# Two chunks' gates of steps 1 to 4 as seven block products, and the matrix operands kept in device memory by product

## What is computed

```python
state = prop_state
for _ in range(5):
    s_in = state @ in_W.T + in_b
    s_out = state @ out_W.T + out_b
    a_in = Af @ s_in
    a_out = AfT @ s_out
    a = concatenate([a_in, a_out, state], axis=-1)
    r = sigmoid(a @ r_W.T + r_b)
    z = sigmoid(a @ z_W.T + z_b)
    joined = concatenate([a_in, a_out, r * state], axis=-1)
    h_hat = tanh(joined @ h_W.T + h_b)
    state = (1.0 - z) * state + z * h_hat
out = tanh(state @ o1_W.T + o1_b) @ o2_W.T + o2_b
return layernorm(x + out)
```

## Time and profile before

| | |
|---|---|
| median of 3 runs | 1029.72 us (1029.61 to 1030.45) |
| the profiled execution, its own time | 1030.75 us |
| its span in the trace | 1028.9 us |
| TensorE busy | 98% of the span, 4648 matmuls |
| VectorE busy | 58% |
| ScalarE busy | 39% |
| share of the chain that ended last that is TensorE | 92% |
| mean granted TensorE clock | 0.99 of full |

### The profile page before, as it was taken

One profiled execution on the slowest core, in us unless ns is written; L12 is line 12 of the kernel. 1 busy time (PEld: TensorE's weight loads), 2 busy tenths in 40 slices (PEclk: granted clock), 3 DMA queues, 4 the chain that ended last, 5 costly groups with the idle time before them and its releaser, 6 DMA issues.

```text
span 1028.9 us, 11463 instructions
## 1 busy us (share of the span) xinstructions
PE 1005.5 (98%) x4648; PEld 458.5 (45%) x4648; DVE 592.3 (58%) x933; ACT 403.8 (39%) x544; POOL 38.7 (4%) x43
## 2 busy tenths in 40 slices
PE   6999999999999999999999999999999999999995
PEld 3444444444444444444444444444444444444443
DVE  4999968895354338544433674353347534446756
ACT  3656665542144126413421552143135314322443
POOL 0311000000000000000000000000000002001100
PEclk8999999999999999999999999999999999999998
DMA  9998991327430244333003642410344335001101
GB/s 330 389 411 344 396 343 33 77 65 218 151 136 0 103 166 91 72 143 143 1 1 143 189 72 72 169 73 0 143 154 72 62 143 189 1 1 42 42 1 41
DMA packets 87236, 134.30 MB, mean 131 GB/s; under 512 B 60432, under 2 KB 75408, under 8 KB 78992
## 3 DMA queue, kind: packets, MB, share of 16 engines
q1 hardware_dynamic: 84880, 125.19, 35.8%
q0 software_dynamic: 2304, 8.39, 2.1%
HBM read 102.11 MB, written 16.78 MB: 116 GB/s over the span
## 4 chain that ended last, share of the span: by engine, by line
PE 92%; DVE 3%; ACT 2%; DMA 1%; issue 1%; SPq 1%; ACTq 0%; DVEq 0%
PE bank L1260 42%; PE bank L1173 36%; PE bank L1116 11%; PE bank L1292 1%; DMA tmp<-in_adj 1%; PE bank L1273 1%; DMA xop_words<-pq_words 0%; SPq L270 0%; DVE pq_words L810 0%; ACT pq_words L468 0%; DVE pq_words L1012 0%; DVE areg L957 0%; ACT pq_words L554 0%; ACT tmp L476 0%; DVE tmp L704 0%
## 5 line engine op out<-in xcount | busy, mean ns | idle before, releaser
L1173 PE MATMUL bank<-areg,xop_words 128*128 128x512 fp8e4 x1792 | 390.1, 379 | 1.4 <-DVE pq_words L1012 1.1
L1260 PE MATMUL bank<-pq_words,w 128*128 128x512 f16 x1440 | 327.3, 379 | 0.0
L1173 PEld LDWEIGHTS bank<-areg,xop_words 128*128 128x128 f16 x1792 | 174.5, 98 | 214.7 <-DVE pq_words L1012 3.1
L1260 PEld LDWEIGHTS bank<-pq_words,w 128*128 128x128 f16 x1440 | 140.9, 98 | 169.9 <-DVE pq_words L1038 0.2
L476 ACT ACTIVATE tmp<-bank,bias_sb,scal 128x512 f32<-128x512 f32 x120 | 93.1, 776 | 201.4 <-PE bank L1260 201.4
L554 ACT ACTIVATE pq_words<-pq_words 128x512 f16<-128x512 f32 x48 | 30.2, 630 | 236.8 <-DVE pq_words L1024 140.5
L831 DVE SCALAR_TENSOR_TENSOR bank<-deg_words,vdeg,bank 128x512 f32<-128x512 f16 x120 | 90.0, 752 | 51.8 <-ACT bank L490 50.7
L1260 PE MATMUL bank<-split,w 128*128 128x512 f16 x480 | 116.7, 379 | 2.4 <-issue 1.9
L1116 PE MATMUL bank<-areg,xop_words 128*128 128x512 fp8e4 x512 | 113.5, 385 | 3.7 <-ACT areg L421 3.7
L490 ACT ACTIVATE bank<-deg_words,vdeg 128x512 f32<-128x512 f16 x120 | 82.7, 691 | 5.2 <-DVE deg_words L794 1.5
L1116 PEld LDWEIGHTS bank<-areg,xop_words 128*128 128x128 f16 x512 | 50.7, 99 | 66.0 <-issue 7.4
(11 more groups left out here) (132 smaller groups left out, 602.9 us busy)
## 6 DMA issues: line engine op xcount, KB each, us to landing
areg<-kept_operands SPq DMA_DIRECT2D x32, 1792.0 KB, 10.6
tmp<-in_adj SPq DMA_DIRECT2D x16, 1024.0 KB, 7.0
tmp<-in_adj_t SPq DMA_DIRECT2D x16, 1024.0 KB, 8.3
kept_operands<-xop_words POOLq DMA_DIRECT2D x11, 512.0 KB, 8.2
areg<-in_x SPq DMA_DIRECT2D x8, 512.0 KB, 8.1
kept_operands<-areg SPq DMA_DIRECT2D x4, 1024.0 KB, 10.2
kept_operands<-tmp POOLq DMA_DIRECT2D x5, 512.0 KB, 3.3
pq_words<-in_gate_w SPq DMA_DIRECT2D x6, 384.0 KB, 6.2
```

The costliest lines, as they stand in the source:

```text
L1173: last = nc.tensor.matmul(dst[:, :], xop[:, m // 2, operand_block(xo, part, m % 2), :], slot8[g % 2][:, m, mo, :], start=first and m == pa ...
L1260: last = nc.tensor.matmul(dst[:, :], w16[:, k, wp, feat(gi)], rhs, start=False, stop=i == KT - 1 and (wp, xp) == PASSES[-1], skip_group_ch ...
```

## The change

For steps 1 to 4, the gates of chunks 0 and 1 are no longer computed tile by tile. Features and chunks make a 2 x 2 block product per gate and direction, which is done as seven products (`pair_gate`, `pair_product`): the left operands are blocks of the gate weights and four sums of them (`ws`), the right ones are `y11`, `y21`, `y22` and the four sums `t1` to `t4` of the y blocks (`yop`). The state's part stays as it was (`pair_state`). `degree_differences`, `weight_full`, `weight_sums`, `weight_hi` and `weight_lo` prepare the sums of the weights and degrees once, in step 1. The scales of all operands change by a factor of 4, and the degree terms with them. Chunks 2 and 3, and step 0, keep the old form; the first seeds of chunk 2 now stand in group 3 of every step.

In `kept_operands` each operand of a group is now one piece of 512 KB, stored in pieces of 512 bytes (the sums with two DMAs for each one before, the rows with three for each two). There is one place for each of the seven operands instead of two slots; SP loads the next group's operand into it when the product that read it has ended. The freed slot holds `yop` and the late chunks' y.

The diff, cut to its core:

```diff
-Y_SPLIT = {False: {"y22": 1, "y12": 2, "y11": 3, "y21": 4}, True: {"y11": 1, "y22": 2, "y12": 3, "y21": 4}}
+Y11, Y21, Y22, YT1, YT2, YT3, YT4 = range(7)
+Y_ORDER = {0: ("y11", "y22", "t1", "t3", "t2", "y21", "t4"), 1: ("y22", "t3", "y11", "t1", "t2", "y21", "t4"),
+           2: ("y22", "y12", "y11", "y21"), 3: ("y22", "y12", "y11", "y21")}
+Y_BASE = (0, 7, 14, 18)
+Y_STEP = 22
+Y_PLACE = {"y11": Y11, "y21": Y21, "y22": Y22, "t1": YT1, "t2": YT2, "t3": YT3, "t4": YT4}
+PAIR_TILES = ((0, 0), (0, 1), (1, 1), (1, 0))
...
-        kept = nc.dram_tensor("kept_operands", (2 * 2, P, PAIRS, NX * CW // 4), F32, kind="Internal").ap()
+        pair_banks = (bank[4:8], (bank_a, bank_b, bank_e, bank_c), bank[4:8])
+        kept = nc.dram_tensor("kept_operands", (2 * 2, NX, P, PAIRS, CW // 4), F32, kind="Internal").ap()
...
+            def load_operand(at, mo, done):
+                if at > 0:
+                    sp.wait_ge(done, at)
+                sp.dma_start(place_w[:, mo, :, :], kept[at % 4][mo]) \
+                    .then_inc(s_place[mo], 16)
+            def load_group(at):
+                load_operand(at, M11, s_p1)
+                load_operand(at, MT2, s_p6)
+                load_operand(at, MT1, s_p5)
+                load_operand(at, MT3, s_p7)
+                load_operand(at, M22, s_p3)
+                load_operand(at, M21, s_p2)
+                load_operand(at, MT4, s_p4)
...
             for t in range(1, STEPS):
-                for g in range(4):
-                    at = 4 * (t - 1) + g
-                    if at + 2 < 4 * LAST:
-                        sp.wait_ge(s_p4, at + 1)
-                        load_group(t + (g + 2) // 4, (g + 2) % 4)
+                for at in range(4 * (t - 1) + 1, 4 * t + 1):
+                    if at < 4 * LAST:
+                        load_group(at)
...
-                to = kept.rearrange("(h d) p m w -> d p h m w", d=2)[d][:, :, m, MT1 * CW // 4:]
                 pool.wait_ge(s_t, i + 1)
-                if i < RING_A:
-                    nc.gpsimd.dma_start(to, ring_a[:, i % 3, :].rearrange("p (h w) -> p h w", h=2)) \
...
+                for h in range(2):
+                    to = kept[2 * h + d, MT1:MT1 + 4, :, m, :].rearrange("s p w -> p s w")
+                    if i < RING_A:
+                        rows = ring_a[:, i % 3, :].rearrange("p (h s w) -> p h s w", h=2, s=4)
+                        nc.gpsimd.dma_start(to, rows[:, h]).then_inc(s_kept_a[i % 3], 16)
...
+            def weight_hi(d):
+                act.wait_ge(s_wsum, 3 * d + 3)
+                nc.scalar.copy(ws[:, d, :, 0, :], w_sums).then_inc(s_wsh, 1)
...
+            def weight_full(d):
+                k = FT * (1 - d)
+                if d == 0:
+                    dve.wait_ge(s_gate, GT * CH)
+                else:
+                    dve.wait_ge(s_wsh, 1)
+                nc.vector.tensor_tensor(w_full, w16[:, k:k + FT, 0, :], w16[:, k:k + FT, 1, :], ALU.add) \
+                    .then_inc(s_wfull, 1)
+            def weight_sums(d):
+                w = w_full.rearrange("p k (r f m) -> p k f r m", r=3, f=FT)
+                a11, a12, a21, a22 = w[:, 0, 0], w[:, 1, 0], w[:, 0, 1], w[:, 1, 1]
+                s1, s2, s3, s4 = [w_sums[:, i, :].rearrange("p (r m) -> p r m", r=3) for i in range(4)]
+                dve.wait_ge(s_wfull, d + 1)
+                nc.vector.tensor_tensor(s1, a21, a22, ALU.add).then_inc(s_wsum, 1)
+                nc.vector.tensor_tensor(s3, a11, a21, ALU.subtract)
+                dve.wait_ge(s_wsum, 3 * d + 1)
+                nc.vector.tensor_tensor(s2, s1, a11, ALU.subtract).then_inc(s_wsum, 1)
+                dve.wait_ge(s_wsum, 3 * d + 2)
+                nc.vector.tensor_tensor(s4, a12, s2, ALU.subtract).then_inc(s_wsum, 1)
+            def weight_lo(d):
+                dve.wait_ge(s_wsh, d + 1)
+                nc.vector.tensor_tensor(ws[:, d, :, 1, :], w_sums, ws[:, d, :, 0, :], ALU.subtract) \
+                    .then_inc(s_wsl, 1)
...
+            def degree_differences():
+                v = vdeg.rearrange("p d (r f) -> p d f r", f=FT)
+                nc.vector.tensor_tensor(vdif[:, :, 0, :], v[:, :, 0, :], v[:, :, 1, :], ALU.subtract).then_inc(s_gdeg, 1)
+                nc.vector.tensor_tensor(vdif[:, :, 1, :], v[:, :, 1, :], v[:, :, 0, :], ALU.subtract).then_inc(s_gdeg, 1)
+                nc.vector.tensor_tensor(degd, deg[:, :, cols(1)], deg[:, :, cols(0)], ALU.subtract).then_inc(s_gdeg, 1)
...
                 if g == 0:
                     y_lo(t, g, "y11")
-                sums_u(at)
+                sums_u(t, g)
+                if t == 1 and g == 1:
+                    weight_full(1)
                 if t == LAST and g >= 2:
                     head_split(g - 2)
-                if t == LAST and g == 3:
+                if g == 3:
                     for gi in range(2):
                         degree_part(CH * t + 2, 2, gi)
                 sums_v(at)
-                y_sum(at, "y22")
+                if t == 1 and g == 1:
+                    weight_sums(1)
+                if g == 1:
+                    for i in range(4):
+                        pair_degree(t, 0, i)
+                y_sum(t, g, "y22")
                 y_lo(t, g, "y22")
-                y_sum(at, "y12")
+                y_sum(t, g, "y12")
+                if g < 2:
+                    if g == 0:
+                        y_sum(t, g, "t1")
+                        y_sum(t, g, "t3")
+                        y_lo(t, g, "t1")
+                        y_lo(t, g, "t3")
+                    else:
+                        y_sum(t, g, "t3")
+                        y_lo(t, g, "t3")
+                        if t == 1:
+                            weight_lo(1)
+                        y_sum(t, g, "t1")
+                        y_lo(t, g, "y11")
+                        y_lo(t, g, "t1")
+                    y_sum(t, g, "t2")
+                    y_lo(t, g, "t2")
+                    y_sum(t, g, "y21")
+                    y_sum(t, g, "t4")
+                    y_lo(t, g, "y21")
+                    y_lo(t, g, "t4")
+                    return
                 y_lo(t, g, "y12")
-                if g > 0:
-                    y_lo(t, g, "y11")
-                if t == LAST and g >= 2:
+                y_lo(t, g, "y11")
+                if t == LAST:
                     residual(g - 2)
-                y_sum(at, "y21")
+                y_sum(t, g, "y21")
                 y_lo(t, g, "y21")
...
             for t in range(1, STEPS):
+                if t == 1:
+                    degree_differences()
+                    weight_full(0)
+                    weight_sums(0)
+                    weight_lo(0)
                 group(t, 0)
                 split_lo(0, split_at(t, 0))
+                split_lo(1, split_at(t, 1))
                 group(t, 1)
-                gates(t, 0)
-                gates(t, 1)
+                pair_gates(t)
                 if t == LAST:
...
+            def pair_product(t, gate, dst, operand, weights):
+                for d in range(2):
+                    if gate == 0:
+                        pe.wait_ge(s_yl, y_done(t, d, [n for n in Y_PLACE if Y_PLACE[n] == operand][0]))
+                        if t == 1 and operand in (Y22, YT1, YT2, YT3):
+                            pe.wait_ge(s_wsl, d + 1)
+                    for wp, xp in PASSES:
+                        last = nc.tensor.matmul(dst[:, :], weights(d, wp), yop[:, d, operand, xp, :], start=False,
+                                                stop=False, skip_group_check=True)
+                return last
...
+            def pair_gate(t, gate):
+                unit, seeds = 3 * (t - 1) + gate, GT * CH * t + 4 * gate
+                slots = pair_banks[gate]
...
+                pe.wait_ge(s_c1, seeds + 1)
+                pair_product(t, gate, slots[0], Y11, block(0, 0)).then_inc(s_gp1, 1)
+                pe.wait_ge(s_c1, seeds + 2)
+                pair_product(t, gate, slots[1], YT2, block_sum(2)).then_inc(s_gp6, 1)
+                pe.wait_ge(s_c1, seeds + 3)
+                pair_product(t, gate, slots[2], YT1, block_sum(1)).then_inc(s_gp5, 1)
+                pe.wait_ge(s_c1, seeds + 4)
+                pair_product(t, gate, slots[3], YT3, block_sum(3)).then_inc(s_gp7, 1)
+                pe.wait_ge(s_gs1, unit + 1)
+                pair_product(t, gate, slots[0], Y21, block(0, 1))
+                pair_state(t, gate, 0)
+                pe.wait_ge(s_g12, unit + 1)
+                pair_product(t, gate, slots[1], Y22, block_sum(4))
+                pair_state(t, gate, 1)
+                pe.wait_ge(s_g22, unit + 1)
+                pair_state(t, gate, 2)
+                pe.wait_ge(s_g21, unit + 1)
+                pair_product(t, gate, slots[3], YT4, block(1, 1))
+                pair_state(t, gate, 3)
...
             for t in range(1, STEPS):
                 first_group(t)
                 group(t, 1)
-                gates(t, 0)
-                gates(t, 1)
```

(34 more changed lines are left out.)

429 lines of the change are left out of this document (321 added, 108 removed).

## The result

The changed kernel takes 1038.42 us (median of 4 runs, 1037.57 to 1039.41) against 1029.74 us before: a ratio of 1.0083 with a 95% interval of 1.0066 to 1.0101. The forecast was 1036.5, slower, for two long waits. The profiled execution takes 1037.57 us (span 1035.8), 6.8 above the profiled one of before.

A forecast was written before the change was run, and what follows sets the result against it. TensorE, busy 98% of the span, bounds the kernel: -15.5 + 4.6 + 1.9 + 2.4 + 9.4 + 4.0 = +6.8 us, so the median goes from 1029.72 to 1036.5 us, range 1032.0 to 1039.8.

The forecast's parts named there:

- What is removed: Gates of chunks 0 and 1, steps 1 to 4: 18 fewer matmuls a step, 72 in all, -15.5 us.
- Start of step 1: Once: TensorE waits for ScalarE's copy of the first product, behind the weights' sums and their rounding; +4.6 us, bounds 3.6 and 5.3.
- Group 1 of step 1: Once: the other direction's weight sums delay splits; gates wait 0.4 for y11 and 1.5 for t2; +1.9 us, bounds 1 and 3.
- Group 0 of each step: Four times: group 1's product 2 waits for the sum y21, 0.6 us each; +2.4 us, bounds 1.2 and 4.
- The end: Step 4, group 3: x rows queued behind the last operand load delay y21, TensorE waits; +9.4 us, bounds 8 and 10.7.
- The clock: Behind the two long waits (step 1, end) TensorE's clock halves, 2.0 us lost each; +4.0 us, bounds 1.6 and 5.
- At nothing: New additions inside the pair gates, the operands' places and the 512-byte stores: all hidden, costing nothing.
- The rival of slow stores: Stores in 512-byte pieces make the last matrix row late: +1.3 to +3.3 us on top, about 1039 us; chance 0.10.
- the clock did not stay up: Rival at the two long waits: the clock stays up, waits cost only themselves; +2.8, 1032.5 us; chance 0.10.
- the gates show no gap: Rival in the pair gates: the 0.4 us lead is gone, 0.3 us missed in each of 12 units; +3.6, 1040 us; chance 0.08.
- faster: Rival at the end: x rows reach y21 under 3.5 us behind group 2's end, saving 11.4; 1025.1 us; chance 0.06.
- break-even: At the end: with the x rows' way to y21 below 9 us behind group 2's end, the change breaks even.

The follow-up runs named there:

- run 5: Changed kernel with the edits of run 1, run 2 and run 3, plus the second direction's full weights and low part made earlier on VectorE: 1015.49 us, ratio 0.9853.
- run 2: Changed kernel, start of step 1: ScalarE copies the first product before rounding the weights' sums, VectorE makes their low part after group 0's splits: 1032.61 us, ratio 1.0036.
- run 3: Changed kernel, VectorE's list of group 0: sum y21 moved ahead of the splits of t1 and t3 and of t2: 1034.68 us, ratio 1.0054.
- run 10: Changed kernel with the edits of run 1, run 2 and run 3 together, without the two further ones of run 5: 1017.07 us, ratio 0.9875.
- Run 4: Kernel before, one wait added in SP's list: bias and x rows issued only when group 2 of step 4 has ended: 1041.38 us, ratio 1.012.
- run 8: Kernel before with the change's operand storage and loads, old gates, x rows behind the last group's loads: 1043.43 us, ratio 1.0129.
- run 7: Kernel before with the change's operand storage and loads, old gates, x rows ahead of the last group's loads: 1030.14 us, ratio 1.0002.
- run 1: Changed kernel, SP's list only: bias and first two chunks' x rows issued ahead of the last group's operand loads: 1024.46 us, ratio 0.9949.
- run 6: Changed kernel with 44 matmuls of unused result added on TensorE before its wait for y21 in group 3 of step 4: 1034.41 us, ratio 1.0044.

## Why the prediction was right, term by term

The sum was +6.8 for the profiled form, and the two profiled executions differ by 6.8. The terms under it were off by up to 1.3 us, and these errors cancelled. So the mechanisms were right and the exact agreement is luck: the second profile of the same kernel takes 1038.31 us, and its clock alone lost 1.15 us more in step 1.

- *What is removed, -15.5.* Right: 4576 matmuls, 46.6 to 42.7 us for a pair's gates, and 15.1 us (13.7 to 16.5) as a time in run 5.
- *Start of step 1, +4.6.* Too high: +3.6 (3.84, less the 0.25 that was there). The place and the chain were as written. The steps of that chain, in the changed kernel:

```profile
240.84 0.60 DVE pq_words L1248
241.45 1.68 DVE tmp L1224
...
243.15 0.56 DVE tmp L1232
...
245.27 0.03 ACT pq_words L639
...
246.65 0.59 ACT pq_words L603
```

  The full weights and the four sums last what I scaled (1.7 and 2.1). The degrees' difference (L1248) holds VectorE for 0.60 where I had 1.15, and ScalarE's rounding starts its successor 1.38 later where I had 1.6. VectorE also came to L1248 0.5 earlier than I counted (240.84 against 241.3). The duration of L1248 is the rule that I set aside for want of a row: by the Trainium skill ("VectorE: DVE Perf Modes", the perf-mode tier table) a `tensor_tensor` with only 16-bit tensors runs at twice the rate. The trace agrees: 0.69 us of busy time for 1024 f16 elements, as long as 512 f32 elements take, against 1.22 for 1024 fp8 elements before.
- *Group 1 of step 1, +1.9.* Of the two waits one came: 1.31 for the split of t2 (predicted 1.5). The 0.4 for y11 did not; it came where edits had let TensorE run earlier (1.06, 0.40 and 1.19 us in runs 2, 3 and 10).
- *Group 0 of each step, +2.4.* 0.48, 0.83, 0.48 and 0.48, 2.3 in all.
- *The end, +9.4.* Mis-sized: +10.7. The chain was the predicted one link for link. The x rows' way was the wrong link: from their issue to GpSimd's start 6.76 us, where I took 4.7, that is 3.9 from an undisturbed transfer and 0.8 for the load ahead. Run 4, with the bias but no operand load ahead, has 5.1 for it; run 8, with the load, 5.8; the last 1.0 came only with the new gates, and its cause is open. So 1.2 of the miss lies in the 3.9 and none in the 0.8. GpSimd's additions came out 0.5 shorter and SP's issues 0.3 shorter than in my sum.
- *The clock, +4.0.* 1.7 and 2.1 (the 12.8 of the end less the wait of 10.7; by the 16 matmuls alone 1.9), 3.8 in all, in this execution. Others gave from 0 to 2.8 for the first wait and 1.3 to 2.7 for the second.
- *At nothing.* The stores, the places and the pair gates' lead: run 7 and run 5 bear it out. A store of 256 KB lands in 7.2 us, one of 512 KB took 8.2. The Trainium skill ("DMA: Bandwidth & Descriptors", Specifications) has 512 bytes as enough for line rate, and run 7 agrees: ratio 1.0002. The pair gates of steps 2 to 4 show no gap (42.7 us in step 2). One thing I had not seen is a new wait ahead of step 0's second half, for a split of VectorE. This row is TensorE's in the changed kernel:

```profile
77.66 53.99 PE L1440 MATMUL bank<-areg,xop_words 128*128 128x512 fp8e4 x244 [1.14 <-DVE pq_words L878]
```

  The chain has an 8.62 us store of `kept_operands` at 60.45 ahead of VectorE's work there, and VectorE waits 0.78 us for it. That wait comes with the new storage: it is there in 8 of the 10 profiles with these stores (0.25 to 1.23 us, 0.83 in run 7 with the old gates) and in neither of the two with the old ones. Whether it reaches TensorE is another matter: TensorE waited 0.61, 0.40 and 0.26 us in runs 1, 3 and 6, in the last two without any wait of VectorE for a store, and not at all in the other six. So the stores explain at most 0.78 of the 1.14, and what the rest is stays open. The slack behind it took it up, as the unchanged start at 138 shows.

The median was missed by 1.9 us. I took the changed kernel's median to lie 1.0 below its profiled form, as before, but the profiled execution was the fastest of its four; no row said that the kernel before's gap would carry over. The rival of slow stores (about 1039) would have given the same median, and the traces and run 7 rule it out: the right number for the wrong reason would have been easy here. Of the other rivals, the clock did not stay up; the gates show no gap beyond the one named; and the condition for "faster" was the right one, x rows that don't hold up y21, as run 1 made it true by SP's list and came out 0.5% faster (1024.46 us, and 1025.1 in the prediction). Its break-even was wrong, though: with 9 us behind T (the end of group 2) the sum is still +2.9; it reaches zero at 6.1, or at 8.1 if the clock's loss at the end goes too.

## What to carry to other kernels

A transfer that stands in a queue behind another has that one's wait too. When a change makes a load wait for a later event, list what is queued behind it: here three small transfers at the end cost 12.8 us, nearly all that 72 matmuls had saved (15.5). In an in-order list, first what the busiest engine waits for, then what prepares later work; all five edits that turned +0.8% into -1.5% only moved instructions in such lists. And price an idle stretch of TensorE that lasts several us at its length plus what the clock may lose behind it, here 1.3 to 2.8 us whenever it fell.

## What the runs showed of the hardware

The clock behind a wait of 3.85 us falls in some executions and not in others. The same 24 matmuls of step 1 took 7.04, 8.19 and 7.98 us in three profiles, and 5.35 in two (runs 1 and 6), with the wait equal to 0.02 us. Behind the waits of 8.7 to 10.8 us it fell in every one of the six profiles that have such a wait, and 16 matmuls took 4.94, 5.53, 5.57, 6.09, 6.31 and 6.37 us against 3.63 behind a wait of 1.34.

One more wait stands in all twelve profiles: 3.33 us in the last output rows, ahead of 24 matmuls of 256 columns. The clock fell behind it in ten of them, the kernel before included (4.11 to 4.46 us), and stayed at full in two (2.79 us, runs 7 and 10). The changed kernel, then run 10:

```profile
1023.31 4.40 PE L1686 MATMUL bank<-o,pq_words 128*128 128x256 f16 x24 [3.33 <-DVE areg L1109]
1003.01 2.79 PE L1698 MATMUL bank<-o,pq_words 128*128 128x256 f16 x24 [3.33 <-DVE areg L1118]
```

So a single profile gives the price of the clock only to about 1.5 us a wait, and a term such as "2.0 for each" wants a range from 0 to 2.8 where the wait is near 4 us. The Trainium skill ("TensorE: Matmul & The Clock Gate", Part 1) says of a kernel's start that the number of slow matmuls differs from run to run; these rows agree, and show the same behind a wait in the middle of a kernel.
